# FFN weights loaded by quarters of their rows and transposed in 32x32 blocks on VectorE, with x2 rows stored in their own order

## What is computed

```python
def reference(x, ctx, Wq, Wk, Wv, Wout, bout, W_r, W_k, W_v, mu_r, mu_k):
    x = x + attention(layernorm(x), ctx)       # sim stretched by 1.5 about its mean, softmax, Wout, bout
    n = layernorm(x)                           # x is called x2 in the kernel from here on
    n_prev = shift_rows_by_one(n)              # zero ahead of each batch
    xr = mu_r * n + (1 - mu_r) * n_prev
    xk = mu_k * n + (1 - mu_k) * n_prev
    r = sigmoid(xr @ W_r.T)
    k = square(relu(xk @ W_k.T))
    return x + r * (k @ W_v.T)
```

## Time and profile before

| | |
|---|---|
| median of three runs | 769.5 us (769.28 to 769.66) |
| the profiled execution: its own time | 770.62 us |
| its span in the profile | 768.3 us |
| mean granted TensorE clock | 0.99 |
| TensorE busy | 745.8 us, 97% |
| VectorE busy | 509.7 us, 66% |
| ScalarE busy | 425.3 us, 55% |
| GpSimd busy | 122.6 us, 16% |
| DMA | 106.78 MB, 44.3% of 16 engines' span in the main queue |

### The profile page before, as it was taken

How to read it: one execution, slowest core, us unless ns; L and a number is a source line. 1 busy time by engine, 2 the same in 40 slices (tenths; PEclk the granted TensorE clock), 3 DMA queues, 4 the chain that set the end, 5 groups by cost and what they waited for, 6 DMA issues and landing times.

```text
span 768.3 us, 13549 instructions
## 1 busy us (share of the span) xinstructions
PE 745.8 (97%) x3966; PEld 651.1 (85%) x3966; DVE 509.7 (66%) x1068; ACT 425.3 (55%) x1199; POOL 122.6 (16%) x280
## 2 busy tenths in 40 slices
PE   7999988999999999999999999999999999999977
PEld 6966868888988989888988989888888989888866
DVE  2557777677767666677767666677766666776651
ACT  2577556464665756465665756465665756464322
POOL 1200011211102021211112121211112121201111
PEclk9999999999999999999999999999999999999998
DMA  9933434443544454443544454443544454442310
GB/s 305 337 117 103 154 101 138 150 136 117 164 131 143 120 171 130 153 138 114 159 130 136 127 171 130 147 140 116 160 129 130 134 171 130 146 132 72 97 55 27
DMA packets 84647, 106.78 MB, mean 139 GB/s; under 512 B 9839, under 2 KB 61321, under 8 KB 84619
## 3 DMA queue, kind: packets, MB, share of 16 engines
q1 hardware_dynamic: 84619, 106.45, 44.3%
HBM read 58.70 MB, written 47.71 MB: 138 GB/s over the span
## 4 chain that ended last, share of the span: by engine, by line
PE 88%; DVE 5%; ACT 2%; DMA 2%; issue 1%; POOL 1%; SPq 0%; POOLq 0%; DVEq 0%; ACTq 0%
PE ffn L456 11%; PE ffn L457 11%; PE ffn L458 11%; PE scores L457 9%; PE scores L458 8%; PE scores L456 8%; PE attended L458 8%; PE attended L457 8%; PE attended L456 8%; PE scores L601 1%; ACT probs L707 1%; PE attended L494 1%; PE attended L493 1%; DVE xk L998 1%; DMA handed<-x_rows 1%
## 5 line engine op out<-in xcount | busy, mean ns | idle before, releaser
L456 PE MATMUL scores<-A_hi,xT_hi 128*128 128x462 f32 (+1 forms) x384 | 134.3, 350 | 0.6 <-DVE xT_lo L891 0.6
L457 PE MATMUL scores<-A_lo,xT_hi 128*128 128x462 f32 (+1 forms) x384 | 134.5, 350 | 0.0
L458 PE MATMUL scores<-A_hi,xT_lo 128*128 128x462 f32 (+1 forms) x384 | 134.1, 349 | 0.0
L707 ACT ACTIVATE probs<-scores,neg_max 128x154 f32<-128x154 f32 x256 | 96.1, 386 | 43.0 <-DVE neg_max L946 38.9
L946 DVE TENSOR_REDUCE neg_max<-scores 128x3 f32<-128x462 f32 (+1 forms) x96 | 55.5, 583 | 90.8 <-PE scores L458 90.8
L456 PE MATMUL attended<-B_hi,pT_hi 128*128 128x512 f32 x288 | 112.8, 392 | 2.9 <-DVE pT_lo L891 2.9
L457 PE MATMUL attended<-B_lo,pT_hi 128*128 128x512 f32 x288 | 113.0, 392 | 0.0
L458 PE MATMUL attended<-B_hi,pT_lo 128*128 128x512 f32 x288 | 112.9, 392 | 0.0
L1188 POOL TENSOR_SCALAR var<-stats 128x1 f32<-128x1 f32 x64 | 12.2, 191 | 466.2 <-DVE stats L897 465.1
L456 PE MATMUL ffn<-xk_hi,WkT_hi 128*128 128x256 f32 x256 | 74.6, 291 | 7.1 <-DVE xk_lo L891 7.1
L456 PEld LDWEIGHTS scores<-A_hi,xT_hi 128*128 128x128 f32 x384 | 72.4, 189 | 8.0 <-issue 0.8
(11 more groups left out here) (160 smaller groups left out, 1524.3 us busy)
## 6 DMA issues: line engine op xcount, KB each, us to landing
prob_rows<-probs SPq DMA_DIRECT2D x32, 704.0 KB, 3.4
probs_handed<-prob_rows SPq DMA_DIRECT2D x128, 176.0 KB, 3.3
x_rows<-normed SPq DMA_DIRECT2D x62, 256.0 KB, 2.0
handed<-x_rows SPq DMA_DIRECT2D x248, 64.0 KB, 1.9
x_in<-in_x SPq DMA_DIRECT2D x32, 256.0 KB, 3.5
out<-x SPq DMA_DIRECT2D x32, 256.0 KB, 2.4
wq<-in_L_xattn_Wq SPq DMA_DIRECT2D x4, 512.0 KB, 8.9
wout<-in_L_xattn_Wout SPq DMA_DIRECT2D x1, 2048.0 KB, 15.7
```

Source lines behind the costliest of these rows:

```text
L456: te.matmul(psum, left[0], right[0], start=first, stop=False)
L457: te.matmul(psum, left[0], right[1], start=False, stop=False)
L458: return te.matmul(psum, left[1], right[0], start=False, stop=last)
L707: last = nc.scalar.activation(probs[:, q, cols], S[b][:, (h - h0) * J:(h - h0 + 1) * J], ACT.Exp, bias=neg_max[:, h:h + 1], accum_out=row_ ...
```

## The change

The three weights are loaded by quarters: partition q*32 + i gets, for each of the 16 groups b of 32 rows, the columns q*128 to q*128 + 127 of row b*32 + i, in pieces of 512 B, four DMAs for a weight. VectorE's new `weights_turn` transposes 32x32 blocks, four instructions of 128x512 for a weight, into `turned_w`, which lies on the weight's low half. `weights_hi` and `weights_lo` read that tile and no PSUM bank. TensorE's `turn_weights` and its waits are gone. Since the rows of x2 are now written in their own order, the columns of its transposed tile come in another order (partition q*32 + i, chunk k is column q*128 + k*32 + i); the transposed W_k and W_r and the vectors `mu` (four DMAs each, the same elements) follow it, and the rows of the k product are placed to fit W_v. Calls move: on ScalarE the high halves of W_k ahead of the exponentials of tile 0, those of W_r to where W_k's were, those of W_v to where W_r's were; on VectorE W_k is transposed ahead of the maxima of tile 0, W_r behind `normalise_late(0)` with all eight low halves of W_k and W_r behind it, W_v behind `probs_lo(1, ...)` with its low halves. `x_lo(1)` and `normalise_late(0)` change places.

```diff
@@ -94,9 +95,11 @@
...
         at_ffn_weights = cursor[0]
-        WT = {}
+        WT, turned_w = {}, {}
         for w in ("k", "r", "v"):
-            WT[w] = (sb(f"W{w}T_hi", [P, DC, D], F32R), sb(f"W{w}T_lo", [P, DC, D], F32R))
+            hi, at_low = sb(f"W{w}T_hi", [P, DC, D], F32R), cursor[0]
+            WT[w] = (hi, sb(f"W{w}T_lo", [P, DC, D], F32R))
+            turned_w[w] = sb(f"W{w}T", [P, DC, D], at=at_low)
         x_in = [sb(f"x_in{i}", [P, D]) for i in range(4)]
@@ -158,9 +161,9 @@
...
         at_raw = at_ffn_weights + 2 * size_of([P, DC, inner])
-        raw_w = {"k": sb("raw_wk", [P, DC, D], at=at_raw),
-                 "r": sb("raw_wr", [P, DC, D], at=at_raw + size_of([P, DC, D])),
-                 "v": sb("raw_wv", [P, DC, D], at=at_act)}
+        raw_w = {"k": sb("raw_wk", [P, 4 * DC, P], at=at_raw),
+                 "r": sb("raw_wr", [P, 4 * DC, P], at=at_raw + size_of([P, DC, D])),
+                 "v": sb("raw_wv", [P, 4 * DC, P], at=at_act)}
@@ -301,7 +304,6 @@
...
         B_BANKS = [T[2], XB, T[0], T[1]]
-        W_BANKS = [T[0], T[1], T[2], XB]
@@ -328,13 +330,20 @@
...
             sp.dma_start(x_in[3][:], xt[3 * P:4 * P, :]).then_inc(x_loaded[3], 16)
-            load_rows(raw_w["k"], W_k, ffn_loaded["k"])
-            load_rows(raw_w["r"], W_r, ffn_loaded["r"])
+            def load_quarters(w, src):
+                rows = src.rearrange("(b i) (q k) -> q i b k", i=Q, q=4)
+                for q in range(4):
+                    sp.dma_start(raw_w[w][q * Q:(q + 1) * Q, :, :], rows[q]).then_inc(ffn_loaded[w], 16)
+            load_quarters("k", W_k)
+            load_quarters("r", W_r)
             sp.dma_start(x_early[:], xt[4 * P:5 * P, :]).then_inc(early_loaded, 16)
-            load_rows(raw_w["v"], W_v, ffn_loaded["v"])
+            load_quarters("v", W_v)
             with nc.allow_non_contiguous_dma(reason="two vectors of 512 as columns"):
                 for w, src in (("k", mu_k), ("r", mu_r)):
-                    sp.dma_start(mu[w][:], src.rearrange("(c p) -> p c", p=P)).then_inc(mu_loaded, 16)
+                    for q in range(4):
+                        part = src[q * P:(q + 1) * P].rearrange("(k i) -> i k", i=Q)
+                        sp.dma_start(mu[w][q * Q:(q + 1) * Q, :], part).then_inc(mu_loaded, 16)
@@ -531,21 +540,6 @@
...
-            def turn_weights(chunks):
-                for n in chunks:
-                    w, c = "krv"[n // DC], n % DC
-                    te.wait_ge(ffn_loaded[w], 16)
-                    if n >= len(W_BANKS):
-                        te.wait_ge(W_ready, n - len(W_BANKS) + 1)
-                    if n == len(W_BANKS):
-                        te.wait_ge(B_ready, FULL)
-                        te.wait_ge(packed_ready, 2)
-                    to = W_BANKS[n % len(W_BANKS)]
-                    for m in range(DC):
-                        last = te.transpose(to[:, m * P:(m + 1) * P], raw_w[w][:, m, c * P:(c + 1) * P], identity[:])
-                    last.then_inc(W_turned, 1)
             def step(g, s):
@@ -649,20 +643,16 @@
...
             turn_x(1)
-            te.wait_ge(vT_ready, 3)
-            turn_weights(range(0, 4))
             scores(1)
             te.wait_ge(wout_loaded, 16)
+            te.wait_ge(vT_ready, 3)
             te.wait_ge(picked_ready, 1)
-            te.wait_ge(W_ready, 4)
             for c in range(BLOCKS):
...
             attend(0)
-            turn_weights(range(4, 8))
             scores(3)
             attend(1)
-            turn_weights(range(8, 12))
             turns(te, step)
@@ -687,8 +677,8 @@
...
                     act_e.wait_ge(x_turned, 2)
-                nc.scalar.activation(by_quarter(normed2), in_quarters(x2[slot]), ACT.Identity, bias=shift2[:],
-                                     scale=rstd2[:]).then_inc(xn2_ready, 1)
+                nc.scalar.activation(normed2[:], x2[slot][:], ACT.Identity, bias=shift2[:], scale=rstd2[:]
+                                     ).then_inc(xn2_ready, 1)
@@ -765,11 +755,11 @@
...
                 w, c = "krv"[n // DC], n % DC
-                act_e.wait_ge(W_turned, n + 1)
+                act_e.wait_ge(W_turned, 4 * (n // DC) + 4)
                 if w == "v":
-                    nc.scalar.mul(WT[w][0][:, c, :], W_BANKS[n % len(W_BANKS)][:], 0.5).then_inc(W_hi_ready, 1)
+                    nc.scalar.mul(WT[w][0][:, c, :], turned_w[w][:, c, :], 0.5).then_inc(W_hi_ready, 1)
                 else:
-                    copy(WT[w][0][:, c, :], W_BANKS[n % len(W_BANKS)][:]).then_inc(W_hi_ready, 1)
+                    copy(WT[w][0][:, c, :], turned_w[w][:, c, :]).then_inc(W_hi_ready, 1)
@@ -835,11 +825,13 @@
...
                      ).then_inc(vT_ready, 1)
+            for n in range(0, 4):
+                weights_hi(n)
             for b in range(3):
...
             normalise_early(0)
-            for n in range(0, 4):
+            for n in range(4, 8):
                 weights_hi(n)
@@ -866,7 +858,7 @@
...
                 probs_hi(1, i)
-            for n in range(4, 8):
+            for n in range(8, 12):
                 weights_hi(n)
@@ -878,8 +870,6 @@
...
                 probs_hi(2, i)
-            for n in range(8, 12):
-                weights_hi(n)
             turns(act_e, step)
@@ -1018,15 +1008,26 @@
...
+            def weights_turn(w):
+                dve.wait_ge(ffn_loaded[w], 64)
+                by_rows = turned_w[w][:].rearrange("p k (b r i) -> p b r k i", r=4, i=Q)
+                mixed_rows = turned_w[w][:].rearrange("p k (r b i) -> p b r k i", b=4, i=Q)
+                for b in range(4):
+                    to = (mixed_rows if w == "k" else by_rows)[:, b]
+                    rows = raw_w[w][:, 4 * b:4 * b + 4, :].rearrange("p r (k i) -> p r k i", i=Q)
+                    v.transpose(to, rows).then_inc(W_turned, 1)
             def weights_lo(n):
-                hi, lo = WT["krv"[n // DC]]
-                bank = W_BANKS[n % len(W_BANKS)]
+                w = "krv"[n // DC]
+                hi, lo = WT[w]
+                full = turned_w[w][:, n % DC, :]
                 dve.wait_ge(W_hi_ready, n + 1)
-                if n // DC == 2:
-                    v.scalar_tensor_tensor(out=lo[:, n % DC, :], in0=bank[:], scalar=0.5, in1=hi[:, n % DC, :].bitcast(F32),
+                if w == "v":
+                    v.scalar_tensor_tensor(out=lo[:, n % DC, :], in0=full, scalar=0.5, in1=hi[:, n % DC, :].bitcast(F32),
                                            op0=ALU.mult, op1=ALU.subtract).then_inc(W_ready, 1)
                 else:
-                    low_part(lo[:, n % DC, :], bank[:], hi[:, n % DC, :]).then_inc(W_ready, 1)
+                    low_part(lo[:, n % DC, :], full, hi[:, n % DC, :]).then_inc(W_ready, 1)
@@ -1113,12 +1114,15 @@
...
             x_statistics(3, 3, 1)
+            weights_turn("k")
             for b in range(3):
...
             inverse_early(0)
+            x_lo(1)
             normalise_late(0)
-            x_lo(1)
-            for n in range(0, 4):
+            dve.wait_ge(A_done, 3 * DC)
+            weights_turn("r")
+            for n in range(0, 8):
                 weights_lo(n)
@@ -1151,7 +1155,8 @@
...
                 probs_lo(1, i)
-            for n in range(4, 8):
+            weights_turn("v")
+            for n in range(8, 12):
                 weights_lo(n)
@@ -1161,7 +1166,7 @@
...
             x2_turn(0, 0, 0)
-            dve.wait_ge(mu_loaded, 32)
+            dve.wait_ge(mu_loaded, 128)
             mix(0, 0, 0)
@@ -1169,8 +1174,6 @@
...
                 probs_lo(2, i)
-            for n in range(8, 12):
-                weights_lo(n)
             turns(dve, step)
```

## The result

The changed kernel takes **773.65 us** in the median of five runs (772.98 to 773.9), the kernel before 769.5 (767.24 to 769.97): ratio 1.0058, 95% interval 1.0042 to 1.0073. It is slower by 4.15 us; 773.5 was forecast. The profiled execution took 773.43 us, with a span of 771.6.

The account below looks back on a forecast made before the run. VectorE and ScalarE work was taken to pace the opening, with TensorE always busy from 121 to 741 us. Terms 3.8 + 3.2 - 2.4 + 1.1 - 1.7 gave +4.0 us: 773.5 against the median, range 770.4 to 778.0.

Parts of the forecast that it names:

- First place: W_r on VectorE: four transposes and eight low parts ahead of `pack_lo(0)`, starting at 52.2 instead of 48.4; +3.8 us.
- Second place: W_v behind `pT_lo` of tile 1: transposes, a wait and low parts take 5.6 us instead of 2.4; +3.2 us.
- Third place: Before `key_columns(0)`: four low parts of W_v leave the VectorE chain; -2.4 us.
- Low clock behind the fifth `values_out`: TensorE's 4.9 us idle brings a restart at 0.50 for 3.4 us; +1.1 us, ends 0 and 2.9.
- Low clock of `key_columns(0)`: TensorE's 2.35 us idle at 115.2 closes, and its low stretch goes; -1.7 us, ends -1.7 and 0.
- The signs: Expected in the changed trace: `pack_lo(0)` near 52.2, tile 1 exponentials 55.7, tile 3 maxima 93 to 94, `key_columns(0)` 123.
- the step on the loads: Weights loaded in 512 B pieces: W_k at 32.2, W_r near 36, W_v near 41, before use; cost 0, ends 0 and +4.
- Costs of 0: Terms counted as 0 us: TensorE's removed transposes, W_k's turn on VectorE, the slower loads, x2's plain write.
- TensorE bounds the opening: Rival: VectorE's chain has slack at 83 and 104, so two removed transpose groups gain; -3.3, 766.2 us; chance 0.12.
- Late weights: Rival: quarters load at only 131 GB/s, W_k lands near 36, tile 0 exponentials slip; 776 to 778 us; chance 0.10.
- The clock gives it back: Rival: no low stretch after the fifth `values_out`, a shorter one at the last tile; +1.2, 770.7 us; chance 0.13.
- longer low stretches: Rival: idles of 4.9 and 6 us bring longer half-rate stretches at two places, +1.7 each; 776.9 us; chance 0.12.

Follow-up runs that it names:

- x2 by quarters: Changed kernel with x2_norm writing by quarters as before, so x2's columns meet other rows of the weights; 773.56 us.
- whole rows: Changed kernel with each weight loaded by one DMA in whole rows of 2 KB, elements lying in other places; 773.53 us.
- transposes put back: Changed kernel with two groups of 16 TensorE transposes added as extra work, behind attend(0) and attend(1); 774.15 us.
- W_v alone moved: Changed kernel with only W_v's transposes and halves moved, around pT_lo of tile 1, the maxima of tile 3 and the first step; 768.34 us.
- 512 B on 128 partitions: Changed kernel with weights loaded in 512 B pieces, each of four DMAs over all 128 partitions, elements in other places; 774.19 us.
- 2 KB on 32 partitions: Changed kernel with weights loaded by four DMAs on 32 partitions each, in whole rows of 2 KB, elements in other places; 773.86 us.
- spread order: Changed kernel with the same instructions, VectorE's and ScalarE's work on the weights moved into their idle stretches; 763.47 us, ratio 0.9923 to the kernel before.

## Why the prediction was right

**The sum.** Forecast +4.0, measured 4.15 between the medians. Term by term, from the table of steps:

- First place, +3.8: 3.7. The mechanism is shown by taking one group away: 2.2 of 2.4 us came back at `pack_lo(0)`, to where ScalarE's `pack_hi` is next.
- Second place, +3.2: 3.2, and moving all 5.6 us away brought 5.3.
- Third place, -2.4: 9.2 at `attend(2)` becomes 6.8 at `key_columns(0)`.
- Low clock behind the fifth `values_out`, +1.1: 2.1 in this trace, where the low stretch lasted over 5.4 us and not the 3.4 of the earlier trace rows. It lay inside the ends that I had set.
- Low clock of `key_columns(0)`, -1.7: 1.5, and there it went as worked out: `gate_rows` ends just as `xk_lo` is ready, TensorE has no wait, and the clock is 1.00.
- Not in the sum: -1.1 from a shorter low stretch at the last tile. I had named it, but only as part of a rival.
- The profiled executions' own starts differ by 0.64 us, which the medians don't show.

**How firm the clock's terms are.** Several experiments leave the work up to `scores(2)` and at the last tile as the changed kernel has it, apart from the loads, so their traces are further executions of the same stretches. All in us; the first and third columns count from the last maximum of tile 0, the last from the last `key_columns` to the last product with the gate.

| trace | `pack_lo(0)` | wait of the fifth `values_out` | `scores(2)` | last tile |
|---|---|---|---|---|
| kernel before | 6.6 | 1.2 | 22.2 | 17.1 |
| changed kernel | 10.3 | 3.4 | 28.1 | 16.0 |
| x2 by quarters | 10.8 | 3.3 | 28.5 | 16.0 |
| whole rows | 10.3 | 4.9 | 26.8 | 16.6 |
| transposes put back | 10.3 | 4.9 | 26.8 | 16.5 |
| W_v alone moved | 10.3 | 4.9 | 26.8 | 16.4 |
| 512 B on 128 partitions | 10.3 | 4.9 | 26.7 | 16.6 |
| 2 KB on 32 partitions | 10.3 | 4.9 | 26.8 | 17.2 |

The added VectorE work is the same everywhere. The clock isn't. In five of the seven traces the fifth `values_out` waits the 4.9 us that were forecast, and the low stretch behind it lasts the 3.4 us that I had taken, here with whole rows:

```profile
59.79 1.93 PE L572 MATMUL ffn<-wout,picked 128*32 128x512 f32 x8 [4.91 <-DVE B_lo L880]
```

```profile
59.80:63.20 3.40, 3.40 (x17) 0.78 (x20) 2.48 (x6) 3.05 (x9) 0.00 (x0) 0.50 0.24 49
```

There it delays `scores(2)` by 0.8 to 0.9 us, not 2.1. In the other two `scores(1)` had run at the low clock, which left 3.4 us of wait, and the next low stretch was longer. The last tile takes 16.0 to 17.2 us with the same work, so the -1.1 isn't an effect of the change either. From the last maximum of tile 0 to the last product with the gate the changed kernel's trace is 3.95 us longer than the one of the kernel before, and 3.6 to 4.4 in the four traces without other work in the opening and in the one with the transposes put back. Of the kernel before there is one trace only, and its execution (770.62) was 1.1 us slower than the median. So VectorE's terms hold, the clock's are right to about 1 us, and that the sum came within 0.2 us is in part luck.

**The signs.** `pack_lo(0)` at 51.43, the exponentials of tile 1 at 54.95, the maxima of tile 3 at 94.37, `scores(4)` with a wait and `key_columns(0)` at 123.7 at full clock are near what was forecast. The idle ahead of `attend(2)` was 4.6 us where nearly 6 was forecast. One sign that was named as proof against the prediction came: `weights_turn("k")` waited 2.24 us for its rows. It proves the step on the loads wrong, and not the sum.

**Costs of 0.** The two groups of TensorE's transposes: shown, within 0.5 us. x2's plain order: shown. The loads: right at the end, within 0.5 us, and wrong on the way. The step reads "One MB then takes 3.9 in place of 2.7 us: W_k at 32.2"; it took 5.3 us (an estimate: 1.05 MB at the 199 GB/s of the row), and VectorE could start at 34.86. I had scaled the rate of hand-overs by their share of busy DMA, but that share reads over 1 here at 199 GB/s. The price was nothing in this trace because ScalarE's exponentials of tile 0, which began at 39.47 behind the high halves in place of 37.9 behind the first maximum, still caught up with the tile's last maximum at 41.6. There was no more room: 0.8 us later at W_k cost 0.5 us at `pack_lo(0)` in the trace with x2 by quarters. SP was 12 us late, not 4, at `store_x(2)`, and `x_turn(2)` had room for it: it ran at 53.9, in its place behind the maxima.

**The rivals.** *TensorE bounds the opening* falls with the transposes put back: 774.15 and no wait ahead of `scores(4)`. *Late weights* falls with whole rows: 773.53. *The clock gives it back* and *longer low stretches* each happened at one place of the changed kernel's trace, the first at the last tile, the second behind `values_out`, and nearly cancelled; in the other traces both are smaller or absent, as the table shows.

**VectorE's block transposes.** The measurement of the changed kernel itself is 0.60 us between starts for 128x512, so 2.5 us a weight. The Trainium skill (VectorE: DVE Perf Modes, "The three transpose paths") would have had 5.0, as estimated from its 311 ns for one 128x128 in bf16; the trace is at half of that. Whether TensorE would be the better place for these transposes in the spread order, as its "Rules for kernel authors" have it, no run shows: 763.47 us was reached with them on VectorE, and the same order with them on TensorE was not run.

## What to carry to other kernels

Before moving work to an engine that is "only 66% busy", find what waits behind the place in its queue: here 12 instructions of 0.6 us stood ahead of one short step, and with the weights' work in the gaps of the same queue that step came 6.1 us earlier (4.2 behind the last maximum in place of 10.3). All of it spread out, the kernel was 0.8% faster than the one before. Price a longer wait of TensorE twice, once as the wait and once as the slower restart behind it. When a queue's order is by hand, look for a step whose input is ready early but which stands behind one that isn't needed yet (`add_x(1)` behind `mix(0)`: 4.2 us, with the moves that went with it). And read a term of the clock from more than one trace before taking it as the change's.

## What the runs showed of the hardware

- A load's rate fell more with the number of partitions that each DMA writes than with its pieces: 388 GB/s (2 KB, 128 partitions), 279 (512 B, 128), 221 (2 KB, 32), 199 (512 B, 32) in the stretch of 29 to 32 us, all in one queue. Over 26 to 38 us the last three are 286, 223 and 211.
- A DMA share above 1 (1.23 at 199 GB/s, 1.06 at 388) isn't a measure of how much data could move.
- Extra work can pay: 32 useless transposes in a wait of 3.4 us kept the granted clock at 1.00 and took 1.3 us off the whole.
- A low stretch behind a wait ahead of the fifth `values_out` cost 0.8 to 2.1 us, and two executions with the same work up to there differed by that much.
- The same wait brings a low stretch in one execution and none in another: behind the 3.6 us ahead of `scores(4)` the clock was 0.59 from 99.6 to 103.4 in the changed kernel, and 1.00 with the wait filled. A wait of 2.24 us ahead of `scores(1)` brought one in the changed kernel, one of 2.22 with whole rows didn't, and one of 2.9 us ahead of the fifth `values_out` didn't either. One execution's stretch is no measure for the next; such stretches are the larger part of what I can't work out beforehand.
- VectorE transposes 128x512 in blocks as fast to a destination with 2 KB between neighbouring blocks (the weights: 0.67 to 0.70 us where one stands alone, 0.60 between starts) as to one with 512 B (the rows of x: 0.69 to 0.70 us).
